# Logits computed once in a second cross-attention, with two layer norms and the first keys given to VectorE

## The reference

```python
x = x + _L0_xattn_ref(_layernorm(x), ctx_1024, ...)   # stage a
x = x + _L0_ffn_ref(_layernorm(x), ...)               # stage b: 6 layers of windowed attention and GEGLU
x = x + _L1_xattn_ref(_layernorm(x), ctx_1024, ...)   # stage c, first part
x = x + _L1_ffn_ref(_layernorm(x), ...)               # stage c, second part: 8 experts, one per token
```

```python
qp = einsum('bld,ed->ble', q, Wq)
idx = argmax(einsum('bld,bmd->blm', qp, kv), -1)
mk, mv = split(take_along_axis(kv, idx[..., None], 1) @ Wkv.T, 2, -1)
qh = qp.reshape(b, l, 16, 8).transpose(0, 2, 1, 3)
logits = einsum('bhld,bmd->bhlm', qh, mk) * scale
attn = softmax(logits, -1)
out = einsum('bhlm,bmd->bhld', attn, mv)              # then times Wc
```

## Time and profile before

| | |
|---|---|
| median of 3 runs | 1940.81 us (1939.25 to 1948.31) |
| profiled execution | 1946.22 us, its span 1944.0 us |
| granted TensorE clock, mean | 0.973 |
| TensorE busy | 1819.9 us, 94% of the span |
| VectorE busy | 1433.7 us, 74% |
| GpSimd busy | 1438.3 us, 74% |
| ScalarE busy | 1140.1 us, 59% |

### The profile page before, as it was taken

One profiled execution on the slowest core, in us unless ns is written; L12 is line 12 of the kernel. 1 busy time (PEld: TensorE's weight loads), 2 busy tenths in 40 slices (PEclk: granted clock), 3 DMA queues, 4 the chain that ended last, 5 costly groups with the idle time before them and its releaser, 6 DMA issues. The chain is left out here.

```text
span 1944.0 us, 78927 instructions
## 1 busy us (share of the span) xinstructions
PE 1819.9 (94%) x32815; PEld 1274.1 (66%) x32815; DVE 1433.7 (74%) x2623; ACT 1140.1 (59%) x2387; POOL 1438.3 (74%) x1838
## 2 busy tenths in 40 slices
PE   7689999999999999999999999999999999789878
PEld 6356667666666666666666766666666666566668
DVE  4587777877787778778777877888778878355556
ACT  2266566656666665666566666656666666334434
POOL 2588779878888888888788888888888879222334
PEclk9799999999999999999999999999999999889979
DMA  3111311111311113111122111121111101030012
GB/s 103 30 52 44 103 49 49 52 45 48 102 54 49 41 47 103 53 45 52 48 67 85 51 41 45 35 88 33 28 35 37 39 24 36 10 100 1 20 44 67
DMA packets 60837, 99.93 MB, mean 51 GB/s; under 512 B 15848, under 2 KB 35065, under 8 KB 58643
## 3 DMA queue, kind: packets, MB, share of 16 engines
q1 hardware_dynamic: 58978, 91.72, 16.3%
q0 software_dynamic: 1504, 3.17, 0.5%
HBM read 44.50 MB, written 21.45 MB: 34 GB/s over the span
## 5 line engine op out<-in xcount | busy, mean ns | idle before, releaser
L1332 PE MATMUL b_bank_proj<-layer_weights,b_stream_t 128*128 128x512 f32 x1152 | 593.7, 617 | 12.5 <-DVE b_plain_moved L1128 9.3
L1128 DVE TENSOR_TENSOR b_plain_moved<-b_bank_proj,b_rope 128x1024 f32<-128x1024 f32 x384 | 467.4, 1221 | 110.3 <-ACT b_squares L962 107.0
L871 POOL TENSOR_TENSOR b_rotated<-b_plain_moved 128x1024 f32<-128x1024 f32 x192 | 453.7, 2363 | 46.5 <-DVE b_plain_moved L1128 46.5
L886 POOL TENSOR_TENSOR b_rotated<-b_rotated,b_inv_norm 128x1024 f32<-128x1024 f32 x192 | 365.5, 1904 | 15.2 <-POOL b_inv_norm L882 0.2
L962 ACT ACTIVATE b_squares<-b_bank_proj 128x512 f32<-128x512 f32 x384 | 229.3, 597 | 248.3 <-PE b_bank_proj L1332 245.3
L1332 PEld LDWEIGHTS b_bank_proj<-layer_weights,b_stream_t 128*128 128x128 f32 x1152 | 188.7, 192 | 115.3 <-issue 53.2
L1134 DVE TENSOR_REDUCE b_norm<-b_squares 128x16 f32<-128x1024 f32 x192 | 232.2, 1209 | 42.7 <-ACT b_squares L962 42.5
L1340 PEld LDWEIGHTS b_bank_shared<-const_tables,b_rotated 128*128 128x128 f32 x1536 | 181.5, 143 | 72.9 <-issue 68.8
L1340 PE MATMUL b_bank_shared<-const_tables,b_rotated 128*128 128x128 f32 x1536 | 213.1, 277 | 3.4 <-POOL b_rotated L886 1.6
L891 POOL TENSOR_TENSOR b_probs<-b_probs,b_inv_sum 128x512 f32<-128x512 f32 x192 | 200.8, 1049 | 14.4 <-DVE b_inv_sum L1149 14.3
L1406 PEld LDWEIGHTS b_bank_shared<-b_attended_t,layer_weights 128*128 128x128 f32 x1536 | 184.2, 193 | 24.9 <-issue 23.2
(11 more groups left out here) (367 smaller groups left out, 2896.7 us busy)
## 6 DMA issues: line engine op xcount, KB each, us to landing
b_v_shifted<-b_v SPq DMA_DIRECT2D x192, 192.0 KB, 2.4
sorted_rows<-sorted_rows SPq DMA_DIRECT2D x66, 258.0 KB, 3.2
layer_weights<-L_ffn_Wqkv SPq DMA_DIRECT2D x6, 1536.0 KB
b_v_shifted<-b_v SPq DMA_DIRECT2D x72, 128.0 KB, 3.0
layer_weights<-L_ffn_Wo SPq DMA_DIRECT2D x6, 512.0 KB
c_sorted_in<-sorted_rows SPq DMA_DIRECT2D x23, 129.0 KB, 2.2
layer_weights<-L_ffn_w SPq DMA_DIRECT2D x8, 256.0 KB, 5.8
c_w<-L_ffn_w SPq DMA_DIRECT2D x8, 256.0 KB, 5.7
```

The source lines that it names most:

```text
L871: nc.gpsimd.tensor_tensor(out=turned[:, k, :], in0=pm[:, k, 0, :], in1=pm[:, k, 1, :], op=ALU.add).then_inc(add_done, 1)
L886: nc.gpsimd.tensor_tensor(out=tk, in0=tk, in1=repeat_last(rn[:, k, :], DH), op=ALU.mult).then_inc(rope_done, 1)
L1128: nc.vector.tensor_tensor(to, src.to_broadcast(shape), tab.to_broadcast(shape), ALU.mult).then_inc(mul_done, 1)
L1332: nc.tensor.matmul(out, xs[:, b, t * P:(t + 1) * P], w, start=True, stop=True).then_inc(proj_full, 1)
```

## The change

1. *Stage a to b.* For the last sequence, statistics, power and normalise move out of stage a into the head of stage b, with tiles and semaphores of their own (`last_*`). TensorE waits for them in `enter(3)`. The rope table on GpSimd waits for its two scale loads alone (`scale_in`).
2. *Last turn of b.* GpSimd's normalise L901 is left out in the last turn; VectorE does it in `norm_t`.
3. *End of b.* `low` and `high` go, with their two memsets and two copies. VectorE makes the keys by head of sequence 0 (`front.kbd`) at the end of `first_counts`; GpSimd's `by_head(0)` goes from stage c.
4. *Stage c.* The second computation of the logits, the transposed maxima and their copies go. VectorE adds the negated maximum to each group of logits, from the PSUM bank into `raised` (128x308 in SBUF); ScalarE takes the exponential there (`exponent`, called where `highest` was); TensorE transposes `raised` (16 transposes for a unit), and ScalarE copies them into `pT`. `logits(u+1)` waits group by group for the adds of unit u.

```diff
-                for b in range(B):
+                for b in range(B - 1):
                     second(b)
...
-                stream(3)
...
+                pool.wait_ge(last_stats, 1)
+                nc.gpsimd.tensor_scalar(last_ve[:, :], last_mv[:, :, 1], EPS, None, ALU.add).then_inc(last_ve_done, 1)
+                pool.wait_ge(last_ve_done, 1)
+                nc.gpsimd.tensor_tensor(out=last_rs[:, :], in0=last_ve[:, :], in1=mhalf[:, 0:TILES], op=ALU.pow).then_inc(last_rstd_done, 1)
+                pool.wait_ge(scale_in, 32)
...
+                    if j == TURNS - 1:
+                        return
                     pool.wait_ge(rstd_done, j + 1)
...
-                    nc.scalar.activation(front.queries, bank[:, :], ACT.Copy)
-                    nc.scalar.activation(front.low[sides[0], :], bank[sides[0], :], ACT.Copy)
-                    nc.scalar.activation(front.high[sides[1], :], bank[sides[1], :], ACT.Copy).then_inc(fq_done, 1)
+                    act.wait_ge(f_set, 2)
+                    nc.scalar.activation(front.queries, bank[:, :], ACT.Copy).then_inc(fq_done, 1)
...
+                before = (B - 1) * SEQ
+                for t in range(TILES):
+                    last = nc.vector.bn_stats(last_st[:, t, :], cols(X, before + t * P, P))
...
                 def norm_t(j):
+                    if j == TURNS - 1:
+                        dve.wait_ge(mv_done, j + 1)
+                        dve.wait_ge(rstd_done, j + 1)
+                        for t in range(TILES):
+                            last = nc.vector.tensor_scalar(xn[:, t, :], xn[:, t, :], mv[:, t, 0:1], rstd[:, t:t + 1],
+                                                           ALU.subtract, ALU.mult)
...
+                    for a in range(2):
+                        nc.vector.tensor_tensor(front.kbd[:, a, :, :], repeat_mid(front.mkd[:, a, :], XHEADS // 2),
+                                                repeat_last(front.own[:, a, :], CTX), ALU.mult)
...
                 def by_head(b):
-                    wait(pool, mkd_done, b)
-                    if b >= 2:
-                        pool.wait_ge(pT_full, 4 * TILES * (b - 1))
+                    pool.wait_ge(mkd_done, b)
+                    if b >= 3:
+                        pool.wait_ge(lg_full, 4 * TILES * (b - 1))
...
-                by_head(0)
...
+                def exponent(u):
+                    for n, g in enumerate((0, 2, 1, 3)):
+                        act.wait_ge(lmax_done, 4 * u + n + 1)
+                        nc.scalar.activation(raised[:, u % 2, g, :], raised[:, u % 2, g, :], ACT.Exp).then_inc(raised_done, 1)
...
-                    nc.scalar.activation(pT[:, u % 2, q, :], bk_t[q % 2][0:CTX, :], ACT.Exp).then_inc(pT_done, 1)
+                    nc.scalar.activation(pT[:, u % 2, (0, 2, 1, 3)[q], :], bk_t[q % 2][0:CTX, :], ACT.Copy).then_inc(pT_done, 1)
...
                 def highest(u):
...
-                        nc.vector.tensor_reduce(nm[:, u % 2, at:at + GROUP], split(bk_l[g][:, 0:GROUP * CTX], CTX), AX.X, ALU.max,
-                                                negate=True).then_inc(lmax_done, 1)
+                        nc.vector.tensor_reduce(largest, group, AX.X, ALU.max, negate=True).then_inc(max_done, 1)
+                        dve.wait_ge(max_done, 4 * u + n + 1)
+                        nc.vector.tensor_tensor(split(raised[:, u % 2, g, :], CTX), group, repeat_last(largest, CTX),
+                                                ALU.add).then_inc(lmax_done, 1)
...
-                def highest(u):
-                    pe.wait_ge(lmax_done, 4 * u + 4)
-                    nc.tensor.transpose(bk_l[0][:, 384:384 + P], nm[:, u % 2, :], ident).then_inc(max_full, 1)
...
                 def probs_t(u, q):
...
-                        last = nc.tensor.matmul(bk_t[q % 2][0:CTX, n * P:(n + 1) * P], kbd[:, b % 2, a, h, :],
-                                                stack(a, b)[:, t * P:(t + 1) * P], start=True, stop=True)
+                        last = nc.tensor.transpose(bk_t[q % 2][0:CTX, n * P:(n + 1) * P], raised[:, u % 2, g, n * CTX:(n + 1) * CTX], ident)
```

More of the change, by code:

```diff
@@ L663, in __init__ @@
         sizes = (("wqT", P), ("wcT", P), ("wkT", XHEADS * XDH), ("wvT", XDH), ("cenT", EXPERTS), ("cT", B * CTX), ("mk", B * CTX),
-                 ("val", B * XDH), ("v32", B * 32), ("mkd", 2 * CTX), ("own", XHEADS), ("queries", SEQ), ("low", SEQ), ("high", SEQ),
+                 ("val", B * XDH), ("v32", B * 32), ("mkd", 2 * CTX), ("own", XHEADS), ("queries", SEQ), ("low", XHEADS * CTX - 4 * P),
                  ("raw", 4 * P), ("cb", B * P), ("z", SEQ), ("one", TILES * CTX), ("pres", CTX),
@@ L682, in __init__ @@
         self.mkd, self.own = split(at["mkd"], CTX), split(at["own"], XHEADS // 2)
-        self.queries, self.low, self.high = at["queries"], at["low"], at["high"]
+        self.queries = at["queries"]
+        begin = sum(n for name, n in sizes[:[name for name, n in sizes].index("low")])
+        self.kbd = wts[:, begin:begin + XHEADS * CTX].rearrange("p (a h j) -> p a h j", a=2, j=CTX)
         self.z, self.sc, self.one = split(at["z"], P), at["z"][:, 0:TILES * CTX], split(at["one"], CTX)
@@ L908, in first_fill @@
                     nc.gpsimd.memset(front.v32, 0.0).then_inc(f_set, 1)
-                    nc.gpsimd.memset(front.low, 0.0).then_inc(f_set, 1)
-                    nc.gpsimd.memset(front.high, 0.0).then_inc(f_set, 1)
                 def first_rstd():
@@ L1114, in _ @@
                 nc.vector.tensor_copy(bands16[:, 1, :, 0, 0, :], band.to_broadcast([P, 2, LOOK])).then_inc(band_set, 1)
+                dve.wait_ge(last_rstd_done, 1)
+                dve.wait_ge(last_stats, 1)
+                for t in range(TILES):
+                    last = nc.vector.tensor_scalar(cols(XS, before + t * P, P), cols(X, before + t * P, P), last_mv[:, t, 0:1],
+                                                   last_rs[:, t:t + 1], ALU.subtract, ALU.mult)
+                last.then_inc(last_done, 1)
                 def mul(u, c):
@@ L1172, in norm_t @@
                 def norm_t(j):
+                    if j == TURNS - 1:
+                        dve.wait_ge(mv_done, j + 1)
+                        dve.wait_ge(rstd_done, j + 1)
+                        for t in range(TILES):
+                            last = nc.vector.tensor_scalar(xn[:, t, :], xn[:, t, :], mv[:, t, 0:1], rstd[:, t:t + 1],
+                                                           ALU.subtract, ALU.mult)
+                        last.then_inc(xn_done, 1)
                     l = j // B
@@ L1596, in gathered_mixture @@
         qpT = m.sb("queries_t", [P, B - 1, SEQ])
-        low = m.sb("low_queries_max", [P, B - 1, SEQ])
-        high = m.sb("high_queries_max", [P, B - 1, SEQ])
+        raised = m.sb("raised", [P, 2, GSIZE, GROUP * CTX])
         sc = m.sb("scores", [P, TILES * CTX])
@@ L1718, in gathered_mixture, with keys_of @@
         maxes = (slice(half, half + SIDE), slice(0, SIDE))
+        def keys_of(b):
+            return kbd[:, b % 2, :, :, :] if b else front.kbd
         def queries_of(b):
             return qpT[:, b - 1, :] if b else front.queries
-        def stack(a, b):
-            return (low, high)[a][:, b - 1, :] if b else (front.low, front.high)[a]
         first = [lot.start for lot in LOTS]
@@ L1972, in rectified @@
                     last.then_inc(ra_done, 1)
-                highest(0)
+                exponent(0)
                 for u in range(LAST + 2):
@@ L2004, in _ @@
                     if u + 1 < NT:
-                        highest(u + 1)
+                        exponent(u + 1)
                     if u < NT:
@@ L2080, in keys @@
                     dve.wait_ge(mkp_done, b)
-                    wait(dve, kbd_done, b)
+                    wait(dve, kbd_done, b - 1)
                     for a in range(2):
```

78 lines of the change are left out of this document (35 added, 43 removed).

## The result

The changed kernel takes 1950.8 us (median of 20 runs, 1942.31 to 1962.57), the kernel before 1942.25 us in the same 20 rounds: ratio 1.0048, 95% interval 1.0034 to 1.0062, so +9.3 us (the two medians alone differ by 8.6), within the 0.5% that I had called no change and at its upper edge. A second comparison gave 1.0051 (1.0033 to 1.0069). The forecast was 1948, +7. The profiled execution of the changed kernel took 1946.29 us, one of its quicker ones.

What follows compares the result with a forecast made beforehand. TensorE was taken as the bound, with VectorE taking its place in attention. Ends and start of c −7.6, walked phases +5.6, clock +9 gave +7 on the median 1940.81: 1948 us, range 1930 to 1963.

Steps and rivals of the forecast that it cites:

- Ends of the stages: End of stage a, −3.9 us from the moved layer norm; last turn of b, −2.0 from the normalise on VectorE.
- Keys by head on VectorE: End of b: two products of 128x616 at 0.77 us each; stage end +0.13, between −0.2 and +0.5.
- Start of c: Stage c up to logits(2): logits(0) no longer waits for GpSimd's keys; −1.8 us, bounds 0 and the 2.8.
- The pair on VectorE: Attention unit: a maximum with its add takes 0.90 us a group, the add 0.48; +2.03 us a unit on VectorE.
- by_token moves behind residual: Plain attention phase: by_token waits for VectorE's residual, starting at +4.9 rather than +5.19; phase 6.6 us where it was 6.92.
- The walk of the phases: Attention phases 1 to 15 walked with 3.67 us of maxima and adds for 1.64: in sum +5.6, between −6 and +19.
- The clock: Attention: pauses make TensorE's clock fall five times at 1.8 us, +9; bounds 0 and 22.
- After the last unit: Phases 14 and 15 walked at −1.0 and −0.5 us; the routing and expert tail behind the last unit the same.
- B: Rival: clock at half in most of the attention stage, seven phases at +3.2, +22 us: 1961; chance .20.
- C: Rival: no new fall of the clock, the bare sum: 1939; chance .15.
- D: Rival: the add overlaps the next maximum, so TensorE's saving of 31 us shows: about 1902; chance .09.
- E: Rival: the adds are dearer, 0.70 us each, 13 us more over 15 units: about 1961; chance .09.

Runs made afterwards that it cites:

- filler: The changed kernel with six matmuls of the identity, that nobody reads, added before by_token: ratio 1.0039 to the kernel before.
- filler_pauses: The changed kernel with unread matmuls of the identity, 8 before counts and 12 before route_t, none elsewhere: ratio 1.0023 to the kernel before.
- logits_only: The changed kernel with the moved last layer norm and the last turn's VectorE normalise undone: ratio 1.0081 to the kernel before, +15.7 us.
- no_add: The changed kernel without the four adds of a unit, its output not the reference's: ratio 0.9888 to the kernel before.

## Why the prediction was right, point by point

- **Ends of the stages, −5.9.** Right: −6.2 and −7.0 measured, and the 3.9 by the rows too.
- **Keys by head on VectorE.** 1.51 us, taken 1.54.
- **Start of c, −1.8.** Wrong in size. From the stage's first instruction to logits(2) the changed kernel takes 17.7 and 17.6 us (before: 18.6), −0.8 and −1.0, inside the bounds of 0 and −2.8. The first maximum came 2.1 us earlier (forecast 2.2). The part lost is in phase 0: 14.2 us, of which 13.6 at half clock, where 5.3 of 11.0 were before. The step expected TensorE to be at half clock "for longer" and it was so for 8 us more. With the last turn and the end of b it is −2.3 and −2.8 (46.8 and 46.3 us from the statistics of the last turn to logits(2); before: 49.1) where my terms make −3.7; but from those statistics to logits(0) ten profiles with the same instructions took 27.6 to 29.2 us, so this part can't be judged more closely.
- **The pair on VectorE, 0.90 a group.** Right: maximum 0.47, add 0.48, one pair every 0.90. The row of the 512-element pair served as the upper bound and L1243's 308 elements were the price. The Trainium skill, "VectorE: DVE Perf Modes", in the section on the errata that put a fixed latency on each instruction, gives an fp32 tensor_tensor of N elements as (N+151)/0.96 ns; for 308 that is 478. The section is about sources in SBUF; here one operand lies in PSUM, and the trace agrees all the same, with 478 to 480.
- **by_token moves behind residual.** Right: the trace names residual as the releaser. In phases 2 and 11 at full clock the last add ended 4.58 us after the phase began and by_token started at 4.92, where the forecast for a plain phase had 4.56 and 4.9.
- **The walk of the phases, +7.1 for 1 to 13.** Right to 0.3 us in every phase that a run shows at full clock but two: it failed in 6 and 10, by 1.0 us each. (For phase 13 the prediction has two figures that don't agree, 6.6 as the plain phase and 7.0 by the walk. The changed kernel never showed it at full clock; filler did, with 7.25 and six more matmuls in it.) There VectorE's normalise of four tiles (L2126, now L2152) moved beside GpSimd's keys by head. The timeline of before:

```profile
1780.08 2.40 POOL L1802 TENSOR_TENSOR c_keys_by_head<-layer_weights 128x616 f32<-128x616 f32 x2 [8.33 <-DVE layer_weights L2083]
...
1782.18 1.15 DVE L2126 TENSOR_SCALAR stream<-residual,c_route_mean_var,c_route_rstd 128x128 f32<-128x128 f32 x4
...
1783.47 0.63 PE L2417 MATMUL c_bank_logits<-const_tables,stream 128*128 128x128 f32 x4 [1.83 <-DVE stream L2126]
```

and of the changed kernel:

```profile
1769.08 2.40 POOL L1836 TENSOR_TENSOR c_keys_by_head<-layer_weights 128x616 f32<-128x616 f32 x2 [11.06 <-DVE layer_weights L2108]
...
1769.95 2.12 DVE L2152 TENSOR_SCALAR stream<-residual,c_route_mean_var,c_route_rstd 128x128 f32<-128x128 f32 x4
...
1772.22 0.63 PE L2443 MATMUL c_bank_logits<-const_tables,stream 128*128 128x128 f32 x4 [2.80 <-DVE stream L2152]
```

  The same four instructions took 1.15 us before, when they came after most of GpSimd's 2.40, and 2.12 us now that they lie within it (2.55 in phase 10, and 2.54 in filler_pauses). One of the four, which takes 0.34 us elsewhere, lasted 1.25: it began inside the second product (1770.26 to 1771.48) and ended 0.08 us after it. The walk moved the instructions and kept their price. TensorE's wait for this normalise is among the waits above (6.4 us in two places, 3.7 before); no run took GpSimd's product away to show it by itself. With phase 8 the other way (12.0 walked, 11.3 seen) the VectorE part comes to about +8.
- **The clock, +9 for five falls at 1.8.** The size agrees with the estimate above (about 9), its make-up was not right, so that the size is luck: 34 and 44 us of half clock spread over nine phases and more rather than five, at 0.2 to 0.3 us for each microsecond of it. I had priced a fall by the work of a phase, but it is cheap wherever VectorE is the one that is late. The sign on TensorE's share missed too: 75% from 1725 to 1860 us and not 60 to 65%; work that half clock stretched counts in it.
- **After the last unit.** The walk gave −1.5 for phases 14 and 15 and left the tail alone; from logits(15) to the end the profiles show 95.9 and 97.0 against 95.1, so +0.8 to +1.9. logits_only gave 94.4. What sets this was not taken apart.
- **The sum.** −3.9, then −2.3 to −2.8, +16.8 to +18.2, +0.8 to +1.9 make +11 to +13 by the profiles, and +9.3 by the runs; the gap is of the size by which stage b differs between two executions. The forecast of +7 is nearer to the runs than its terms are to the profiles: the start of c, the walk and the part behind logits(15) all came out dearer than forecast.
- **Rivals.** Half clock in most of the stage (B) didn't come: 34 to 44 of 132 us. Nor did a stage without a fall (C); the granted clock fell below 1.00 in every phase from 5 to 13 of the first profile. The forecast that no add hides (against D) was right, and the add at 0.70 (E) wrong. For B stood what the prediction had from the Trainium skill, "TensorE: Matmul & The Clock Gate", Part 4: PE-mode transpose, that transposes don't count as activity in the same way. Phases 1 to 4 of the first profile kept a clock of 1.00 with 16 transposes in each (the second had 3.4 us of half clock in 2 and in 3), and the fall came with the pauses of 2 to 4 us in phases 5 to 10; the fillers, which are plain matmuls, took away most of it. Phase 0, at half clock nearly throughout, looks like the page's case, but no_add has the same transposes and was back at 1.00 12.1 us after the start of the stage, the kernel before at 12.8, the changed one at 17.1. Whether as many transposes as filler would have held the clock was not tried.

## What to carry to other kernels

Taking work from the bound engine pays only up to the slack of the one that gets the rest: here some 2 us a unit were taken from TensorE (by the prediction's rows) and 2.0 put on VectorE, which had 2.3 spare in a plain phase and less in those with statistics and picks; the same edit without the new adds measured 31 us less. When an engine that drove a stage begins to wait, price the clock along with the wait, and look for pauses that can be filled; but a filler must stand only where the pause is. And when a walk moves an instruction in time, look up what GpSimd does at its new place before keeping its duration.

## What the runs showed of the hardware

- A normalise of four 128x128 tiles from SBUF on VectorE took 1.11 to 1.12 us alone and 2.12 to 2.55 where GpSimd's product of 128x616 ran beside it for 1.5 to 2 us: an instruction of it that met the product ended 0.08 to 0.09 us after the product did. The Trainium skill, "GPSIMD Engine Reference", 1. Specifications, says that GpSimd shares its SBUF interfaces with VectorE and names instructions in a 2-port mode and those with two SBUF inputs as the ones that suffer; the trace agrees in that this instruction waits, and shows nothing of its mode. The add from PSUM kept its 478 to 480 ns beside GpSimd's normalise of the token rows (11 of 64 places); none of the 64 fell beside the product.
- Plain matmuls whose result nobody reads kept the granted clock up: 34 to 44 us of half clock became 14 us with 6 before by_token, 21 with 8 and 12 in the long pauses, and 7 with 6, 10 and 12 in all three places.
- Half clock can be free: 3.4 us of it in phase 3 left its 7.91 us unchanged.
- Two profiles of one kernel differed by 5 to 9 us at the end of stage b, and twelve profiles of the same stage by up to 17 us, with 31 to 51 us of half clock in it; that the clock is the cause is argued from the two going together.
